# A score tile of key block 3 that spans both query halves, with new order tables

## The chip, the cores and the metric

One NeuronCore of one Trainium2 chip. The metric is device time in microseconds (us) of one execution. The program is straight-line: five engines (TensorE = PE, VectorE = DVE, ScalarE = ACT, GpSimd = POOL, and SyncE = SP, which issues all transfers) each run their own list of instructions in order, and semaphores join them.

## The reference

A block of a transformer on x of 8 x 1024 x 256, all in float32: half a feed-forward part, attention, the same half feed-forward again.

```python
x = x + 0.5 * ffn(layernorm(x))
x = x + attn(layernorm(x))
x = x + 0.5 * ffn(layernorm(x))
```

The feed-forward part is `x @ W.T + b` plus a low-rank part of 8 experts of rank 16, of which a softmax gate keeps the best two. The attention has 16 heads; queries and keys have 16 content dimensions and 32 rotary ones, values have 16. Keys and values come from a latent of 64 that is normalised by its root mean square; scores are scaled by 1/sqrt(48), masked causally and put through a softmax; the output is multiplied by W_o.

## The kernel before, in words

**Tiles.** Tokens are handled in 16 halves of 512 (two per batch). Work before attention (feed-forward, latents, queries and keys) and after it (output projection, feed-forward) is cut into 32 jobs. 30 of them run in lane 0; the second and the last run in lane 1, whose buffers are carved out of `probs` and whose PSUM banks are `o_b` and one bank of `st_b`. Attention is cut into 32 groups (`quads`), each four heads of one batch.

**One group.** `mx` (L807) computes scores with queries on the partitions; DVE takes their row maxima (L998 for tiles on the diagonal, with a mask added, and L1001). When a half's 16 rows of maxima are folded, `mx_turn` transposes them on PE (L813), DVE negates them (L1016), and SP copies them to DRAM (L651) and back (L655) as one extra row of the query operand, the row of shifts. `score` (L775, L777) then computes the transposed scores, keys on the partitions, in two matmuls per head and tile: the second adds the low-order parts of the keys. The row of shifts subtracts each query's maximum. ACT takes the exponential out of `st_b` into the ring `probs` (L884), POOL zeroes the 128 x 128 corner of each tile on the diagonal (L1199), and `pv` (L795) multiplies by the values into `o_b`, four heads side by side. DVE transposes and divides (L1023 to L1036), and SP stores the result (L667).

**The list of score tiles.** `ATT` has for each query half h2 and key block j a tile of the queries from q0 on, n columns: half 0 has n = 512, 384, 256, 128 for j = 0 to 3; half 1 has 512 for j = 0 to 4, then 384, 256, 128. A score matmul is never narrower than 256 columns (`WIDE`): a tile of 128 is computed 256 wide and only its last 128 columns are used. `PV` joins the tiles in pairs, 6 value products a group. `PLACE` gives each tile its place in the ring of 2304 columns, and `BEFORE` the older tile whose value product must be done before it is overwritten.

**What sets the order.** `ORDER` holds a string per engine; each letter takes the next step of one stream (`STREAMS`): on PE S score, X mx, V pv, F mx_turn, P a piece of queries or keys, J and j a job's matmuls, D and d a fill matmul on the identity (L862). The maxima of group g+1 are computed while the scores of group g run. Each engine waits at the head of its own list, so what stands behind a waiting instruction waits too. With two banks, a score waits for the exponential of the score before last (L771), and a maximum matmul for DVE's maximum before last (L806).

**The end.** After the last score of group 31 PE has the y matmuls of the last lane 0 job (L732, L734), the last value product, fill, and then the last job, in lane 1: its output projection is in two parts, the first (L693) on the 128 rows of attention output that the early load (L593) brings, the second (L701) on the rest.

Of the kernel before, what the change touches and what calls it, by code (L numbers as in the profile page):

```python
# [130 lines left out]
def uses(*steps):  # L131

    out = []
    for n, (m, pair, side) in enumerate(UNIT):
# [1139 lines left out]
```

## Time and profile before

| what | value |
|---|---|
| median of 3 runs | 1963.67 us (1953.01 to 1965.78) |
| the profiled execution | 1961.27 us, span 1959.6 us |
| mean granted clock of PE | 0.984 of 2.4 GHz |
| instructions | 32772 |
| busy: DVE, ACT, POOL | 1434.8, 1013.1, 858.1 us |
| moved by DMA | 307.50 MB, mean 157 GB/s |

The span runs from the first to the last instruction of the profiled execution; its time contains 1.7 us around it. Busy times are of that one execution. A PE row's duration runs from its start to the end of its pipeline, so the durations of neighbours overlap, and the starts tell the pace. Idle time of an engine that nobody waits for costs nothing.

### The profile page before, as it was taken

What the parts mean: (1) busy time and instruction counts of PE and PEld (TensorE: products, weight loads), DVE (VectorE), ACT (ScalarE), POOL (GpSimd) and SP (SyncE); (2) the same over time, 40 slices, a digit from 0 to 9 for tenths busy, and PEclk for the clock granted to TensorE, in tenths of its full rate; (3) what the DMA queues carried; (4) which work ended last, traced back from release to release, by engine and by line L of the source; (5) the groups of instructions that cost most, each with busy time, mean ns of one, the idle gap of its engine ahead of it and who ended that gap; (6) DMA issues with size and microseconds to landing.
All of it is one profiled execution on the core that took longest, in us unless ns stands there. A gap on an engine that the chain in (4) does not pass through costs nothing.

```text
span 1959.6 us, 32772 instructions
## 1 busy us (share of the span) xinstructions
PE 1901.9 (97%) x11102; PEld 1337.0 (68%) x11102; DVE 1434.8 (73%) x4570; ACT 1013.1 (52%) x2125; POOL 858.1 (44%) x912
## 2 busy tenths in 40 slices
PE   8789999999999999999999999999999999999997
PEld 7546666767767676776767677677766777677556
DVE  5667777777777777877877777777778778677632
ACT  3435565555555555555555555545555555554551
POOL 3456454543445435355452545535444543432121
PEclk9879999999999999999999999999999999999999
DMA  3775675676775656766666676755677566665611
GB/s 104 199 191 155 166 188 151 151 187 167 176 177 129 178 149 159 200 157 153 162 164 152 179 189 156 179 149 153 153 189 178 143 158 174 167 147 129 133 41 44
DMA packets 169767, 307.50 MB, mean 157 GB/s; under 512 B 15104, under 2 KB 33792, under 8 KB 169600
## 3 DMA queue, kind: packets, MB, share of 16 engines
q1 hardware_dynamic: 169600, 305.40, 62.3%
q8 instruction: 89, 1.46, 0.3%
q14 instruction: 78, 0.64, 0.1%
HBM read 178.99 MB, written 126.22 MB: 156 GB/s over the span
## 4 chain that ended last, share of the span: by engine, by line
PE 86%; DVE 8%; ACT 3%; issue 2%; DMA 1%; POOL 1%; SPq 0%; POOLq 0%; DVEq 0%
PE st_b L775 15%; PE mx_b L807 15%; PE st_b L777 13%; PE o_b L795 13%; PE tp_b L843 5%; PE wj_b L732 5%; PE tp_b L840 4%; PE wj_b L719 3%; PE wj_b L701 3%; PE wj_b L734 2%; PE wj_b L712 2%; PE wj_b L741 1%; PE wj_b L747 1%; DVE mx_b L998 1%; ACT probs L884 1%
## 5 line engine op out<-in xcount | busy, mean ns | idle before, releaser
L884 ACT ACTIVATE probs<-st_b 128x512 f32<-128x512 f32 (+3 forms) x1536 | 699.6, 490 | 582.2 <-PE st_b L777 535.8
L998 DVE CUSTOM_DVE_ANT_0 mx_b<-mx_b,tri 128x256 f32<-128x256 f32 (+3 forms) x1024 | 510.6, 516 | 123.8 <-PE mx_b L807 120.5
L775 PE MATMUL st_b<-st 97*128 97x512 f32 (+2 forms) x1536 | 587.7, 388 | 8.5 <-ACT probs L884 5.0
L807 PE MATMUL mx_b<-st 96*128 96x256 f32 (+2 forms) x1536 | 543.2, 400 | 23.8 <-DVE mx_s L998 14.3
L777 PE MATMUL st_b<-st,k_st 96*128 96x512 f32 (+2 forms) x1536 | 531.2, 350 | 0.0
L1001 DVE TENSOR_REDUCE mx_s<-mx_b 128x1 f32<-128x512 f32 (+1 forms) x512 | 334.3, 653 | 131.8 <-PE mx_b L807 126.5
L1199 POOL TENSOR_SCALAR_AFFINE_SELECT probs<-probs 128x512 f32<-128x512 f32 x256 | 172.2, 677 | 538.1 <-ACT probs L884 538.0
L807 PEld LDWEIGHTS mx_b<-st 96*128 96x128 f32 x1536 | 280.9, 192 | 181.1 <-issue 73.4
L775 PEld LDWEIGHTS st_b<-st 97*128 97x128 f32 x1536 | 291.4, 190 | 123.8 <-issue 54.7
L777 PEld LDWEIGHTS st_b<-st,k_st 96*128 96x128 f32 x1536 | 294.2, 192 | 37.1 <-issue 13.9
L795 PE MATMUL o_b<-probs,v_s 128*17 128x512 f32 (+3 forms) x3072 | 290.3, 496 | 0.0
L795 PEld LDWEIGHTS o_b<-probs,v_s 128*17 128x17 f32 x3072 | 71.1, 97 | 144.8 <-issue 116.1
L998 DVE DVE_READ_ACCUMULATOR2_ANT mx_s<- 128x1 f32 x1024 | 143.6, 140 | 0.0
L527 POOL TENSOR_TENSOR rot<-rot,cos_t 128x512 f32<-128x512 f32 x62 | 80.4, 1297 | 124.4 <-ACT rot L897 124.3
L897 ACT ACTIVATE rot<-tp_b 128x512 f32<-128x512 f32 x124 | 74.1, 598 | 106.8 <-PE tp_b L843 60.6
L732 PE MATMUL wj_b<-w_s,xt 128*128 128x256 f32 x480 | 124.2, 381 | 1.1 <-ACT xn L976 1.1
L1222 POOL TENSOR_TENSOR xa<-xa,hb_s 128x256 f32<-128x256 f32 x120 | 92.7, 799 | 57.7 <-DVE xn L1107 57.7
L843 PE MATMUL tp_b<-stg,wkr_s 128*128 128x512 f32 x240 | 114.3, 598 | 0.8 <-ACT v_s L897 0.6
L1162 DVE SCALAR_TENSOR_TENSOR xa<-wj_b,xa 128x512 f32<-128x512 f32 x60 | 41.5, 692 | 95.0 <-PE wj_b L734 94.9
L732 PEld LDWEIGHTS wj_b<-w_s,xt 128*128 128x128 f32 x480 | 88.5, 190 | 14.4 <-ACT xn L976 3.2
L840 PE MATMUL tp_b<-stg,wq_s 128*128 128x512 f32 x180 | 92.3, 593 | 0.0
L1051 DVE TENSOR_TENSOR lo_t<-rot,hi_t 128x1024 fp32r<-128x1024 f32 x62 | 81.7, 1318 | 9.4 <-ACT hi_t L932 9.2
(198 smaller groups left out, 2332.7 us busy)
## 6 DMA issues: line engine op xcount, KB each, us to landing
st<-q_scratch SPq DMA_DIRECT2D x128, 384.0 KB, 6.0
st<-k_scratch SPq DMA_DIRECT2D x128, 384.0 KB, 8.7
k_st<-k_scratch SPq DMA_DIRECT2D x128, 384.0 KB, 9.2
q_scratch<-hi_t SPq DMA_DIRECT2D x32, 768.0 KB, 3.8
q_scratch<-lo_t SPq DMA_DIRECT2D x32, 768.0 KB, 5.3
k_scratch<-hi_t SPq DMA_DIRECT2D x30, 768.0 KB, 6.1
k_scratch<-lo_t SPq DMA_DIRECT2D x30, 768.0 KB, 4.9
ao_scratch<-o_f SPq DMA_DIRECT2D x252, 32.0 KB, 1.8
```

The costliest lines, as they stand in the source:

```text
L732: nc.tensor.matmul(dst, xt[:, tk, P * kk:P * kk + P], w1_s[:, kk, 0:D], start=(kk == 0), stop=False)
L775: nc.tensor.matmul(dst, k1_st[u][0:SHIFT + 1, a, P * j:P * j + P], q_st[u][0:SHIFT + 1, a, q0:q0 + w], start=True, stop=False)
L777: nc.tensor.matmul(dst, k2_st[0:SHIFT, a, P * j:P * j + P], q_st[u][0:SHIFT, a, q0:q0 + w], start=False, stop=True).then_inc(st_full, 1)
L795: last = nc.tensor.matmul(o_b[32 * a:32 * a + DV + 1, 0, q0 - HALF * h2:q0 - HALF * h2 + n], v_s[g // NQ % 2][:, j, HQ * q + a, :], probs[ ...
L807: nc.tensor.matmul(mx_b[:, m % 2, 0:w], q_st[u][0:SHIFT, a, P * i:P * i + P], k1_st[u][0:SHIFT, a, k0:k0 + w], start=True, stop=True).then ...
L840: last = nc.tensor.matmul(dst, wq_s[:, k, eight], own.stg[:, :, 2 * P:3 * P], start=True, stop=True)
L843: last = nc.tensor.matmul(dst, wkr_s[:, kk, k, eight], own.stg[:, :, P * kk:P * kk + P], start=(kk == 0), stop=(kk == KD - 1))
L884: nc.scalar.activation(probs[:, a, PLACE[s]:PLACE[s] + n], st_b[:, a % 2, HALF - n:HALF], ACT.Exp, scale=SCALE).then_inc(exp_done, 1)
L998: nc.vector.tensor_tensor_reduce(src, src, tri[:, HALF - n:HALF], 1.0, NEG, ALU.add, ALU.max, dst).then_inc(mx_done, 1)
L1001: nc.vector.tensor_reduce(dst, src, AX_X, ALU.max).then_inc(mx_done, 1)
L1199: nc.gpsimd.affine_select(out=d, in_=d, compare_op=ALU.is_ge, fill=0.0, base=0, pattern=[[0, HQ], [1, P]], channel_multiplier=-1).then_inc ...
L1222: last = nc.gpsimd.tensor_tensor(own.xa[:, k, :], own.xa[:, k, :], hb_s[:, :], ALU.add)
```

## The change

The two tiles of key block 3 that stood for half 0 (128 columns, computed 256 wide) and half 1 (512 columns) are cut anew: the first has 256 columns, the last 128 queries of half 0 and the first 128 of half 1, the second the other 384. The second moves up to right behind key block 0's tile of half 1 (`ATT.insert(HT + 1, ...)`). The third value product of a group takes three sets of columns now (`TAKES`): block 0, the second half of the spanning tile, and the 384. The places in the ring follow. The first score of the spanning tile also waits for half 1's row of shifts. The order tables of all five engines are made anew: before, one string for the whole program; now a head, a batch of 4 groups that is repeated 4 times, and a tail. 25 of the 135 fill matmuls are gone, and the last job's projection waits for the reading of `o_b` and the last exponential. Lane 1's carved buffers may reach up to column 1920 of the ring (1792 before).

The diff, with one row of the tables, PE's second, for all:

```diff
--- before.py
+++ after.py
@@ -47,11 +47,18 @@
+BOTH = HT - 1
 ATT = []
 for h2 in range(2):
     for j in range((h2 + 1) * HT):
         q0 = max(P * j, HALF * h2)
-        ATT.append((h2, j, q0, HALF * (h2 + 1) - q0, q0 == P * j))
+        if j == BOTH:
+            q0 += P * h2
+        ATT.append((h2, j, q0, HALF * (h2 + 1) - q0 + (P if j == BOTH and not h2 else 0), q0 == P * j))
+at = [s for s in range(len(ATT)) if ATT[s][0] and ATT[s][1] == BOTH][0]
+ATT.insert(HT + 1, ATT.pop(at))
 NS = len(ATT)
 UNITS = NS * HQ
 DIAG = [s for s in range(NS) if ATT[s][4]]
@@ -66,9 +73,16 @@
     BEFORE.append(max(over))
 PV = [(s, s + 1) for s in range(0, NS, 2)]
 NV = len(PV)
-PV_OF = [p for p in range(NV) for _ in PV[p]]
+TAKES = []
+for p in range(NV):
+    takes = [(s, ATT[s][0], ATT[s][2], min(ATT[s][3], HALF * (ATT[s][0] + 1) - ATT[s][2])) for s in PV[p]]
+    if p == HT // 2:
+        takes.insert(1, (BOTH, 1, HALF, P))
+    TAKES.append(takes)
+PV_OF = [max(p for p in range(NV) if s in [take[0] for take in TAKES[p]]) for s in range(NS)]
 PV_END = [max(p for p in range(NV) if ATT[PV[p][1]][0] == h2) for h2 in range(2)]
@@ -143,122 +157,80 @@
 ORDER = {
     "PE": (
...
-        "JjPJPDPXXPXPXXXPXXJXPXJXXPJXXPXXPFPXXXXXXXXXPXXPJXJXXSSXXSSXXSSPXXSSXXSXSXSVXXPXSSXPXSXSSXXXPXXXXXXXVXXF"
...
+        "JjPJPDPXXPXPXXXPXXJXPXJXXPJXXPXXPFPXXXXXXXXXPXXPJXJXXSSXXSSXXSSPXXSSXXSXSXSVXXPXSXPXXXXXPXXXXXXXXXFXXPXX"
...
 }
@@ -688,6 +660,8 @@
                     late = n == NJ - 1
                     if late and k == 0:
                         pe.wait_ge(ao_early, 16)
+                        pe.wait_ge(o_read, 2 * QUADS)
+                        pe.wait_ge(exp_done, UNITS * QUADS)
                         for tk in range(GT):
                             c = D * (tk % 2)
                             nc.tensor.matmul(wj_of(n, f"wo{tk // 2}")[:, c:c + D], aoc[:, 0, P * tk:P * tk + P],
@@ -762,6 +736,8 @@
                     i = UNITS * g + HQ * s + a
                     if j == 0 and a == 0:
                         pe.wait_ge(shift_in[u][h2], 16 * (g // 2 + 1))
+                    if s == BOTH and a == 0:
+                        pe.wait_ge(shift_in[u][1], 16 * (g // 2 + 1))
                     if j == HT * h2 and a == 0:
                         pe.wait_ge(k2_in[h2], 32 * (g + 1))
                     if g < 2 and s == 0 and a == 0:
@@ -789,11 +765,11 @@
                         pe.wait_ge(o_read, 2 * g + half)
                     if p == 0 and q == 0:
                         pe.wait_ge(tp_free, tp_use("v", 2 * (g // NQ) + 1, 1) + 1)
-                    for s in PV[p]:
-                        h2, j, q0, n, _ = ATT[s]
+                    for s, h2, q0, n in TAKES[p]:
+                        j, place = ATT[s][1], PLACE[s] + q0 - ATT[s][2]
                         for a in range(HQ):
                             last = nc.tensor.matmul(o_b[32 * a:32 * a + DV + 1, 0, q0 - HALF * h2:q0 - HALF * h2 + n],
-                                                    v_s[g // NQ % 2][:, j, HQ * q + a, :], probs[:, a, PLACE[s]:PLACE[s] + n],
+                                                    v_s[g // NQ % 2][:, j, HQ * q + a, :], probs[:, a, place:place + n],
                                                     start=(j == 0), stop=(s == PV[PV_END[h2]][-1]))
                     last.then_inc(pv_done, 1)
                 elif name == "mx":
```

Line numbers of the new kernel are smaller: score is L751 and L753, mx L783, pv L771, mx_turn L789, the fill L838, the projection L667 and L675, y L706 and L708, the v matmuls L832 (L856 before).

**PE, fourth and fifth score tiles of group 16.** 256-column pairs are the tiles of key blocks 2 and 3, 512 those of block 0 for half 1. Before, from the middle of the fourth tile on:

```order
L775 MATMUL st_b<-st 128x256 [waits exp_done]
L777 MATMUL st_b<-st,k_st 128x256
L775 MATMUL st_b<-st 128x256 [waits exp_done]
L777 MATMUL st_b<-st,k_st 128x256
L807 MATMUL mx_b<-st 128x384 [waits mx_done,qk_in11]
L775 MATMUL st_b<-st 128x512 [waits exp_done,shift_in01]
L777 MATMUL st_b<-st,k_st 128x512
L775 MATMUL st_b<-st 128x512 [waits exp_done]
L777 MATMUL st_b<-st,k_st 128x512
L807 MATMUL mx_b<-st 128x256 [waits mx_done]
L807 MATMUL mx_b<-st 128x384 [waits mx_done]
L813 MATMUL tp_b<-ident,mxf 72x128 [waits tp_free,mx_folded]
```

Now, from the first score of the spanning tile on:

```order
L751 MATMUL st_b<-st 128x256 [waits exp_done,shift_in01]
L753 MATMUL st_b<-st,k_st 128x256
L783 MATMUL mx_b<-st 128x512 [waits mx_done]
L751 MATMUL st_b<-st 128x256 [waits exp_done]
L753 MATMUL st_b<-st,k_st 128x256
L783 MATMUL mx_b<-st 128x384 [waits mx_done,qk_in11]
L751 MATMUL st_b<-st 128x256 [waits exp_done]
L753 MATMUL st_b<-st,k_st 128x256
L751 MATMUL st_b<-st 128x256 [waits exp_done]
L753 MATMUL st_b<-st,k_st 128x256
L783 MATMUL mx_b<-st 128x256 [waits mx_done]
L751 MATMUL st_b<-st 128x512 [waits exp_done,shift_in01]
```

The wait for half 1's row (`shift_in01`) stands at the spanning tile's first score now, four heads earlier than before; the tile keeps its 256 columns. Behind these rows the tile of block 3 for half 1, formerly four pairs of 512 three tiles further on, follows with four pairs of 384.

**PE, last scores of group 14 and first of group 15.** `kv_hl`, `kv_lh` are the weights of the v matmuls. Before:

```order
L777 MATMUL st_b<-st,k_st 128x256
L807 MATMUL mx_b<-st 128x256 [waits mx_done] x2
L856 MATMUL tp_b<-kv_hl,kvs 128x256 [waits tp_free]
L856 MATMUL tp_b<-kv_lh,kvs 128x256
L856 MATMUL tp_b<-kv_hl,kvs 128x256
L856 MATMUL tp_b<-kv_lh,kvs 128x256
L775 MATMUL st_b<-st 128x512 [waits exp_done,k2_in0,shift_in10]
L777 MATMUL st_b<-st,k_st 128x512
L775 MATMUL st_b<-st 128x512 [waits exp_done]
L777 MATMUL st_b<-st,k_st 128x512
L807 MATMUL mx_b<-st 128x256 [waits mx_done]
```

Now:

```order
L753 MATMUL st_b<-st,k_st 128x256
L783 MATMUL mx_b<-st 128x256 [waits mx_done] x2
L771 MATMUL o_b<-probs,v_s 17x512 [waits masked]
L771 MATMUL o_b<-probs,v_s 17x512 x3
L771 MATMUL o_b<-probs,v_s 17x384 x4
L751 MATMUL st_b<-st 128x512 [waits exp_done,k2_in0,shift_in10]
L753 MATMUL st_b<-st,k_st 128x512
L751 MATMUL st_b<-st 128x512 [waits exp_done]
L753 MATMUL st_b<-st,k_st 128x512
L783 MATMUL mx_b<-st 128x256 [waits mx_done] x2
```

Behind the two maxima matmuls of 256 columns stood the v matmuls; now a value product of 512 and 384 columns stands there, and the v matmuls come after the next two maxima matmuls.

**PE, the end: last value product and what follows it.** `o_b<-probs,v_s` is the value product, `wj_b` the y matmuls, `wo_s` the projection. Before:

```order
L732 MATMUL wj_b<-w_s,xt 128x256 [waits wj_free]
L732 MATMUL wj_b<-w_s,xt 128x256
L734 MATMUL wj_b<-bt_s,xn 128x256
L732 MATMUL wj_b<-w_s,xt 128x256 x2
L734 MATMUL wj_b<-bt_s,xn 128x256
L795 MATMUL o_b<-probs,v_s 17x256 [waits masked]
L795 MATMUL o_b<-probs,v_s 17x256 x3
L795 MATMUL o_b<-probs,v_s 17x128 x4
L862 MATMUL mx_b<-ident 128x128 [waits mx_done] x26
L693 MATMUL o_b<-wo_s,probs 128x256 [waits ao_early,wj_free_2]
L693 MATMUL o_b<-wo_s,probs 128x256
L693 MATMUL st_b<-wo_s,probs 128x256 x2
```

Now, from the last row of the value product on:

```order
L771 MATMUL o_b<-probs,v_s 17x128 x4
L706 MATMUL wj_b<-w_s,xt 128x256 [waits wj_free]
L706 MATMUL wj_b<-w_s,xt 128x256
L708 MATMUL wj_b<-bt_s,xn 128x256
L706 MATMUL wj_b<-w_s,xt 128x256 x2
L708 MATMUL wj_b<-bt_s,xn 128x256
L706 MATMUL wj_b<-w_s,xt 128x256 [waits wj_free]
L706 MATMUL wj_b<-w_s,xt 128x256
L708 MATMUL wj_b<-bt_s,xn 128x256
L706 MATMUL wj_b<-w_s,xt 128x256 x2
L708 MATMUL wj_b<-bt_s,xn 128x256
L667 MATMUL o_b<-wo_s,probs 128x256 [waits o_read,exp_done,ao_early,wj_free_2]
```

The value product stood behind the y matmuls, followed by 26 fill matmuls; now it stands ahead of them, one fill matmul stands a few rows earlier, and the projection (`o_b<-wo_s,probs`, L667) follows the y matmuls at once.

**SP, the end.** The transfers of the last job. Before:

```order
L600 DMA aoc<-ao_scratch 128x2x512 [waits wj_full,ao_out]
L606 DMA out_y<-xa 128x4x256 [waits wj_free]
L580 DMA probs<-x_scratch 128x1024 [waits stored,pv_done,normed_1_2,stored_2]
L664 DMA probs<-o_f 16x512 [waits o_ready]
L664 DMA probs<-o_f 16x512 x3
L593 DMA probs<-ao_scratch 128x512 [waits pv_done,ao_out]
L594 DMA probs<-ao_scratch 64x512
L606 DMA out_y<-probs 128x4x256 [waits wj_free_2]
```

Now:

```order
L572 DMA aoc<-ao_scratch 128x2x512 [waits wj_full,ao_out]
L552 DMA probs<-x_scratch 128x1024 [waits stored,pv_done,normed_1_2,stored_2]
L565 DMA probs<-ao_scratch 128x512 [waits pv_done,ao_out]
L566 DMA probs<-ao_scratch 64x512
L636 DMA probs<-o_f 16x512 [waits o_ready]
L636 DMA probs<-o_f 16x512 x3
L578 DMA out_y<-xa 128x4x256 [waits wj_free]
L578 DMA out_y<-probs 128x4x256 [waits wj_free_2]
```

The load of x for the last job and the two early loads (`probs<-ao_scratch`) have moved ahead of the four small transfers (`probs<-o_f`), and lane 0's last store behind them.

## Rows read from the trace of the kernel before

**Rows 1.** Page, part 1: busy us, share of the span, instructions of each engine.
```profile
PE 1901.9 (97%) x11102; PEld 1337.0 (68%) x11102; DVE 1434.8 (73%) x4570; ACT 1013.1 (52%) x2125; POOL 858.1 (44%) x912
```

**Rows 2.** Page, part 4: chain that ended last, share of the span by engine.
```profile
PE 86%; DVE 8%; ACT 3%; issue 2%; DMA 1%; POOL 1%; SPq 0%; POOLq 0%; DVEq 0%
```

**Rows 3.** Groups by form, PE: shapes, count | busy us, mean ns | idle before.
```profile
L775 PE MATMUL st_b<-st 97*128 97x512 f32 x768 | 327.7, 427 | 4.5 <-ACT probs L884 2.2 <-issue 1.2
L777 PE MATMUL st_b<-st,k_st 96*128 96x512 f32 x768 | 306.2, 399 | 0.0
...
L775 PE MATMUL st_b<-st 97*128 97x384 f32 x256 | 98.6, 385 | 0.3 <-ACT probs L884 0.2
...
L777 PE MATMUL st_b<-st,k_st 96*128 96x384 f32 x256 | 86.8, 339 | 0.0
```

**Rows 4.** Time line, PE, middle: start us, us, engine, line, what, count.
```profile
1002.42 0.40 PE L775 MATMUL st_b<-st 97*128 97x512 f32 x1
...
1003.35 0.34 PE L807 MATMUL mx_b<-st 96*128 96x384 f32 x1
...
1007.91 0.84 PE L795 MATMUL o_b<-probs,v_s 128*17 128x256 f32 x16
...
1013.28 1.91 PE L795 MATMUL o_b<-probs,v_s 128*17 128x512 f32 x16
...
1028.83 0.34 PE L775 MATMUL st_b<-st 97*128 97x384 f32 x1
...
1029.53 0.40 PE L847 MATMUL tp_b<-kvs,kv_hl 128*128 128x512 f32 x1
...
1049.53 1.70 PE L795 MATMUL o_b<-probs,v_s 128*17 128x512 f32 x16
```

**Rows 5.** Time lines; last row a stretch: us, busy of five engines, PEclk, DMA.
```profile
750.89 0.39 PE L807 MATMUL mx_b<-st 96*128 96x256 f32 x1 [1.80 <-DVE mx_s L998]
...
1213.43 0.39 PE L807 MATMUL mx_b<-st 96*128 96x256 f32 x1 [0.57 <-DVE mx_s L998]
...
1675.83 0.38 PE L807 MATMUL mx_b<-st 96*128 96x256 f32 x1 [1.77 <-DVE mx_s L998]
...
747.34 0.69 DVE L1132 TENSOR_TENSOR k1m<-iota,ixf 128x32 f32<-128x32 f32 x1
...
1944.65 0.19 DVE L1132 TENSOR_TENSOR probs<-iota,probs 128x32 f32<-128x32 f32 x1
...
747.25 2.10 POOL L1222 TENSOR_TENSOR xa<-xa,hb_s 128x256 f32<-128x256 f32 x3
...
751.80:755.20 3.40, 3.40 (x14) 1.66 (x16) 2.15 (x11) 1.79 (x3) 1.64 (x2) 0.50 1.00 297
```

**Rows 6.** Time line, PE, first group of heads.
```profile
151.02 0.49 PE L807 MATMUL mx_b<-st 96*128 96x512 f32 x1 [0.46 <-DVE mx_s L998]
```

**Rows 7.** Time lines of the end: POOL, PE, and the DMA queue's issues.
```profile
1915.91 0.63 POOL L1199 TENSOR_SCALAR_AFFINE_SELECT probs<-probs 128x512 f32<-128x512 f32 x1 [1.40 <-ACT probs L884]
...
1915.83 1.10 PE L732 MATMUL wj_b<-w_s,xt 128*128 128x256 f32 x4 [0.54 <-ACT xn L976]
...
1921.17 0.84 PE L795 MATMUL o_b<-probs,v_s 128*17 128x256 f32 x16
...
1930.17 1.10 PE L693 MATMUL o_b<-wo_s,probs 128*128 128x256 f32 x4 [2.15 <-DMA probs<-ao_scratch]
...
1924.39 2.51 SPq L664 DMA_DIRECT2D probs<-o_f  x4
```

**Rows 8.** Last group: transposed maxima, copy of the row, first score; landings of L651.
```profile
1871.29 0.30 PE L813 MATMUL tp_b<-ident,mxf 128*72 128x128 f32 x1
...
1873.44 0.56 SPq L655 DMA_DIRECT2D st<-shift_scratch  x1
...
1882.41 0.28 PE L775 MATMUL st_b<-st 97*128 97x256 f32 x1
...
DMA to landing us min/median/max: 1.3/2.7/7.5
```

More of the change, by code:

```diff
@@ new lines @@
+        "EEEEEJEEEEEEEEEEEEEEEEEJEEJEEJEEJEECEECEJCHEEEECEECEEJJEEJEEJEECEEJEEHEECEEJEECEEEEEEEECEECEECEEEEEHEEEE"
+        "EJEEJEECJEEJEEJEECEEEEJEECEEEEHEEEEEEEEEEEEJEEJEEJEEJEECEECEEJEECEEHEEEECEECEECJEEJEEJEEJEEHJEEEECEECEEJ"
+        "EEEEEEEECEEEECEECEEEEEEHEEECEECEEJEEJEEJEEJEECEEHJEEEE",
+        "EEEEEJEEEEEEEEEEEEEEEEEJEEJEEJEEJEECEECEJCHEEEECEECEEJJEEJEEJEECEEJEEHEECEEJEECEEEEEEEECEECEECEEEEEHEEEE"
+        "EJEEJEECJEEJEEJEECEEEEJEECEEEEHEEEEEEEEEEEEJEEJEEJEEJEECEECEEJEECEEHEEEECEECEECJEEJEEJEEJEEHJEEEECEECEEJ"
@@ L211 @@
+        "EEEEEEEECEEEECEECEEEEEEHCEECEECEEEEEEHEEEEEEEEEEEEEEEEJEEJEEJEEJEEJEEEEEEEEEEEEJEEEEEEEEEEEEEEEEEEEEEEEE"
+        "EEEEJEEJEEJEEJEEJEEEEEEEEEEEEJEEEEEEEEEEEEEEEEEEEEEEEEEEEEEEEEEEEEEEEEEEEEEEEEEEEEEEEEEEEEEEEEEEEEEEEEEE"
+        "EEEEEEEEEEEEEEEEEEEEEEEEEEEEEEEEEEEEJJEEJJEEJEEEEEEJjjjjjj",
     ),
@@ L238 @@
[L238 to L241 removed]
+        "MMMMLMMJMJMMMMMMMLMMMMMMLMMMMMMMMMLMMfMMMMMMLMMMnMMMMMLMMfnMMMMJLMMJMMoMMooMMoMLMMMMMMJMMJLMMJMMJMMJMJMM"
+        "LMfnJMMJMMJJMMLJJJMMJoJoJMMoMMoMJMMMMfMMJnMMJMJMMLMMJLMMJMMoJoMMooMMMMMMMMMMMMMMLLMMfnJMMJMMMMJMJJMMoJMM"
+        "ooMMoMMLMLfJMMJnMMMMMoMMooMMoMMLMMMLMMMMMMMMMMMMMMMMLfJnMMJJJJJJJMMJJMMLMMoMMoMMooMMMMfMJMMLLMnMoMMoJMMM"
@@ new lines @@
+        "oMMoJJMMJMMMJMMJMMMMMMMMMMMJMMJfMMnJMMoMMoooJMMJMMJMMJJMMMMLMMfMLMMJnMMJoMMoMoMMoMMMMMMJMJJJJMMJMMJLMJLJ"
+        "MMJMMMMMMfJnMMJMMMMMMoMMooMMoMMLMMfMMMJMMJMJLMMJnMMJoMMoMMooMMMMMMMJMJJJJMMJJJJJMMMMLMMLJMMfJnMMJJJMMMMJ"
+        "MMJMMoMMooMoMMMMfJMMJnMMMJMMMMMMLJMMoMMoooLMMJJMMJJMMJMJMMMMLMMMMMMfJLJnJMMJJJJJJJMMMMMMMMJMMJMMoMofoMMo"
+        "nMMMJMMJMJMMLoMMoooMMJMMLMMJMMMMMMMMMMMMJMJMJfJLJMMJLnJJM",
+        "MJJMMooMoMoMJMMJMMJJMMJMMfMJMMnJMMoMMooMMoMMMMJMMJMMMMJMMLJMMJMMJJMMJLMMJJMMfnMMJMMJMMJJLJJJMMJJJMMLMMoM"
@@ new lines @@
+        "MoooJMMfJMMnMMMMMMMMLMMJMMJoJMMooJMMJMMoMMLMMMMMMJJJJJMMJJJJJMMfnMMMMMMLJMMLJJMMJoMMJMMoJJMMoMMfoMnMMMMM"
+        "JMMJMMMMJMMLJMMoooLMMoJMMJJJMMJJMMLMMMMMMMfJJJJLnMMJJJJJJMMMMMMMMJMMJMMoMofoMMonMMMMMJMJMMLJMMoooMMoJMML"
+        "MMJMMMMMMMMMMMMJMJMJfJLJMMJLnJJM",
+        "MJJMMooMoMoMJMMJMMJJMMJMMfMJMMnJMMoMMooMMoMMMMJMMJMMMMJMMLJMMJMMJJMMJLMMJJMMfnMMJMMJMMJJLJJJMMJJJMMLMMoM"
+        "MoooJMMfJMMnMMMMMMMMLMMJMMJoJMMooJMMJMMoMMLMMMMMMJJJJJMMJJJJJMMfnMMMMMMLJMMLJJMMJoMMJMMoJJMMoMMfoMnMMMMM"
@@ L262 @@
+        "sJqaJkuussaqkuusJsqkaJJssuauqkuusksqJJassauuqkusu",
+        "sqakJsJsJaqkuussquuaksJsJuaquksqsJuukasJsJuuaqkuusksqJJassauuqkusu",
+        "sqakJsJsJaqkuussquuaksJsJuaquksqsJuukasJsJuuaqkuusksqJJassauuJqkususqakssaJJJqkssqakssaJJqksqsakssaksksa"
+        "aJjjaJj",
     ),
```

145 lines of the change are left out of this document (39 added, 106 removed).

## Prediction

> **What bounds the kernel now.** I read the engine shares first: TensorE (PE) is busy 97% of the span [rows 1]. The chain that ended last says the same: 86% of it is PE work, 8% VectorE (DVE), 3% ScalarE (ACT) [rows 2]. So a column removed on PE is worth its own time wherever PE isn't waiting in that stretch. Where PE does wait I looked at its time line: a recurring spot in the middle [rows 5], the first group of heads [rows 6], and the last 45 us, one long chain [rows 7].
>
> **Score columns.** Key block 3 had two score tiles: 128 useful columns for query half 0, computed 256 wide, and 512 for half 1. Now they are 256 and 384 wide. The first costs what it did; the second loses 128 columns in 2 matmuls for each of 4 heads and 32 groups: 128 pairs (L775, L777) go from the 512 to the 384 form. By mean durations a pair falls from 427 + 399 to 385 + 339 ns, so 102 ns [rows 3], times 128 = 13.1 us. By starts in the time line, two 512 pairs take 1003.35 - 1002.42 = 0.93 us, two 384 pairs 1029.53 - 1028.83 = 0.70 us [rows 4]: 0.115 us a pair, times 128 = 14.7 us. I take 14.0: durations overlap between matmuls and starts don't, but not every pair stands back to back. The lower end is 0, if PE then waits for exponentials or maxima instead.
>
> **Exp, mask, value product.** The exponentials keep their total of columns (128 + 512 becomes 256 + 384) and their count, and hide behind PE, which is at 97%: nothing; without that cover it would still be nothing. The mask still works on 128 columns of each diagonal tile. The value product of key block 3 for half 1 is now two sets, 128 columns out of the first tile and 384 out of the second: 128 more matmuls in the program, the same columns. Does a split cost? 512 + 512 columns take 1.91 us, 512 + 384 take 1.70, 256 + 128 take 0.84 [rows 4]. So 128 columns are worth 0.21 us, and 1.70 - 4 x 0.21 = 0.86 us agrees with the 0.84 us of the group that has a 128-column set in it: a short set costs its columns alone, 0. The upper end charges each of the 32 groups one step of 0.21 us more, +6.7 us.
>
> **The new wait.** Key block 3's first tile now waits for half 1's row of shifts, one tile earlier than it was needed, with all of PE behind it. In the last group, where the way is shortest, the maxima are transposed at 1871.29, the row's copy is issued at 1873.44 (0.56 us), and that tile starts at 1882.41 [rows 8]. A write of these maxima lands after 2.7 us in the median; if the row takes as long it is there at 1876.7, 5.7 us early. Cost 0; the upper end is rival C.
>
> **First group of heads.** There the tile can't stand before the shift any more. The order puts its four score pairs and one value product behind the transposition. They lay in a stretch in which PE waited for DVE's maxima (0.46 us at 151.02, [rows 6]); now they stand where PE is full: 4 pairs of 256 columns (a 512 pair of 0.465 us less 2 x 0.115 = 0.235 us) plus 0.84 us = +1.8 us. Ends 0 and +5: PE may also be granted the low clock there, as after the waits of rows 5.
>
> **The end.** The y matmuls of the last lane 0 job (from 1915.83) stand ahead of the last value product, though its operand was masked by 1915.91 + 0.63 = 1916.54; it runs at 1921.17 [rows 7]. Behind it come DVE's division, four small issues from 1924.39 (2.51 us), the early load issued behind them, and at 1930.17 the output projection, which waited 2.15 us for that load. The new order has the value product first, the y matmuls in place of 26 fill matmuls, and the early load ahead of the four. Step by step: value product 1916.6 to 1917.4; the four issues 2.4 us later, as now (1921.17 + 0.84 to 1924.39), so 1919.8 to 1922.3, and the last one lands some 2 us after its issue, near 1923.8; the early load is issued near 1918.5 and took 1930.17 - 1926.90 = 3.3 us, so it is there by 1921.8. PE: y matmuls 1917.4 to 1922.7 (they took 1921.17 - 1915.83 = 5.3 us), then at once the projection, against 1930.17: -7.5 us, of which I count 7.4. All behind it is the same. Ends -4 (the four transfers land 3 us later) and -8.
>
> **The recurring spot.** At 750.89 PE has waited 1.80 us for DVE [rows 5], which is late because small routing operations take long (L1132 0.69 us at 747.34, 0.19 us at 1944.65) while GpSimd adds biases (2.10 us from 747.25). Right after it PE is granted 0.50, which is 1.2 GHz, for 3.4 us: 1.7 us lost. Such a wait is there five times, every 232 us, from 750.89 to 1675.83; the least, 0.57 us at 1213.43, had no low clock behind it. At four times 1.80 + 1.7 and once 0.57 it costs some 14 us.
> The page SBUF — State Buffer of the Trainium skill, section Who interferes with whom, says that a DVE instruction with two SBUF inputs contends with a GpSimd instruction that reads SBUF, and that the later one is blocked. The trace agrees: both sides have two SBUF inputs here.
> In the new order DVE has a similar run, but behind the two maxima matmuls PE has a value product of 1.70 us, where four v matmuls of 256 columns (0.12 us each, half a 256 pair) stood. That covers 1.2 of the 1.8 us and leaves a wait like that at 1213.43. If nothing like it arises elsewhere the gain is some 12 us; a new table can make such spots anew, which its order alone doesn't tell. I take half, -6; ends -14 and +8 (two or three new ones a batch).
>
> **Sum.** -14.0 - 7.4 + 1.8 - 6 = -25.6 against the profiled execution's 1961.3: 1935.7. That execution lies 2.4 us under the median of 1963.67, so I say 1938; its own range is 1930 to 1946.
>
> **Rivals.**
> A: nothing is won at the recurring spots: -19.6, so 1944; with new ones 1952. For it: the same runs of routing operations are still there. Against: more cover at the known spot.
> B: the scores' gain turns into waits for maxima and exponentials: the sum without the 14.0, 1952. For it: [rows 5] and [rows 6] show PE paced by DVE. Against: those are single places; PE is 97% busy.
> C, the other side: the shift row is late, at the first score of key block 3 in each group. The longest landing seen is 7.5 us [rows 8]; a copy out and a copy back of that length make at most 17.7 us from transposition to tile (2.15 + 7.5 + 0.56 + 7.5), 6.6 more than the 11.1 us of the last group. At 1.5 us in each of 32 groups it is +48: 1986. It decides from 25.6 / 32 = 0.8 us a group. Against: the median landing leaves 5.7 us.
> D: PE falls to the low clock at the end, now that 26 fill matmuls are gone. The y matmuls of the last job (5.3 us) and some 3 us of transpositions and products on that chain would double: +8, 1946. Against: y matmuls fill the place, and the wait of 2.15 us goes.
> The page TensorE: Matmul & The Clock Gate of the Trainium skill, section HAM oscillation, says that a kernel whose PE idles between bursts drops to half rate and pays for it each time; by that rule taking fill away is a risk, and the time would be D's. The trace agrees at the recurring spots.
>
> **Chances.** Forecast 0.54, A 0.24, B 0.10, D 0.07, C 0.05. A measurement of this kernel can tell about 1% from no change, so faster means under 1944.0. That takes 0.52 of the forecast's 0.54, 0.12 of A, 0.02 of B and 0.03 of D, rounded to 0.70; same is 0.25, slower 0.05 (C). The range is 1926 (the spots all gone) to 1954 (A with new ones, and B).
>
> **What would show it.** The 384-column form of both score matmuls counts 384 instead of 256, the 512 form 640, with means as they are. The projection starts right behind the y matmuls, some 29 us before the end, with no wait for the early load. No wait of 1.8 us every 232 us and no clock of 0.50 in the middle. No wait ahead of key block 3's first tile. I am wrong if PE's waits and low clocks in the middle grow, or if that tile waits for a transfer.

## The result and the profile after

The changed kernel takes 1933.22 us (median of 6 runs, 1930.2 to 1939.6) against 1963.82 for the kernel before beside it (6 runs): ratio 0.9859, 95% interval 0.9836 to 0.9882. Forecast were 1938 and 1926 to 1954. Its profiled execution took 1934.2 us, span 1932.5. Two later groups of runs gave 0.987 (0.9839 to 0.9901) and 0.9861 (0.9837 to 0.9884). Three single executions of later runs (3659.8 us in e0, 3040.9 in e2, 2111.6 in e6) were slow ones and are left out of ratios and medians.

I cut both spans at the same marks, the starts of the last score matmul of groups 0, 7, 27 and 31. Two views of the stretches, first the kernel before, then the changed one (us, length, then busy time and count of PE, PEld, DVE, ACT, POOL, then PE's granted clock, DMA share, GB/s):

```profile
0.00:190.80 190.80, 164.70 (x787) 115.36 (x788) 126.39 (x397) 83.07 (x144) 93.51 (x100) 0.91 0.58 161
190.80:573.50 382.70, 379.79 (x2242) 262.56 (x2240) 295.53 (x931) 212.66 (x449) 180.99 (x188) 0.99 0.67 169
573.50:1731.40 1157.90, 1143.92 (x6754) 809.29 (x6752) 886.57 (x2816) 618.23 (x1315) 543.15 (x566) 0.99 0.67 166
1731.40:1914.80 183.40, 178.49 (x1080) 118.62 (x1080) 114.22 (x387) 95.57 (x210) 34.71 (x51) 0.99 0.45 98
1914.80:1959.60 44.80, 34.98 (x249) 31.22 (x247) 12.14 (x45) 3.59 (x9) 5.73 (x8) 0.97 0.15 48
```

```profile
0.00:192.20 192.20, 165.27 (x794) 114.57 (x795) 126.51 (x397) 82.44 (x143) 93.14 (x97) 0.91 0.59 159
192.20:574.80 382.60, 376.79 (x2299) 262.40 (x2297) 296.18 (x928) 214.52 (x451) 183.91 (x191) 1.00 0.68 169
574.80:1712.80 1138.00, 1129.16 (x6913) 810.01 (x6913) 888.89 (x2821) 622.89 (x1315) 536.92 (x566) 1.00 0.66 168
1712.80:1896.60 183.80, 178.70 (x1109) 120.38 (x1107) 113.93 (x384) 95.96 (x209) 33.62 (x51) 0.98 0.46 102
1896.60:1932.50 35.90, 29.55 (x202) 26.01 (x200) 12.14 (x45) 3.86 (x9) 6.45 (x9) 0.99 0.18 59
```

The gain is in two places: the middle, groups 8 to 27, 1157.9 to 1138.0 us (PE busy 14.8 us less, idle 5.1 less), and the end, 44.8 to 35.9. Groups 1 to 7 and 28 to 31 gain nothing, although scores got narrower there too. The forms of the scores, which answer to [rows 3] (count | busy us, mean ns | idle before):

```profile
L753 PE MATMUL st_b<-st,k_st 96*128 96x512 f32 x640 | 254.6, 398 | 0.0
...
L751 PE MATMUL st_b<-st 97*128 97x384 f32 x384 | 144.4, 376 | 1.1 <-ACT probs L860 1.0
...
L753 PE MATMUL st_b<-st,k_st 96*128 96x384 f32 x384 | 130.1, 339 | 0.0
```

128 of each moved from 512 to 384 columns, at the means of before (the first score matmul has 376 ns for 385). The recurring spot, which answers to [rows 5]: PE's time line and the same stretch of clock.

```profile
751.76 0.76 PE L783 MATMUL mx_b<-st 96*128 96x256 f32 x2 [0.38 <-DVE mx_s L974]
```

```profile
751.80:755.20 3.40, 3.40 (x22) 3.16 (x23) 2.81 (x12) 2.34 (x6) 1.37 (x2) 1.00 1.01 230
```

The wait is 0.37 or 0.38 us at all five spots, where it was 1.80, 1.77, 0.57, 1.52 and 1.77, and the clock stays 1.00. The end, which answers to [rows 7] (PE, then SyncE's issues):

```profile
1904.15 1.03 PE L667 MATMUL o_b<-wo_s,probs 128*128 128x256 f32 x4
...
1905.88 1.03 PE L675 MATMUL o_b<-wo_s,probs 128*128 128x256 f32 x4
```

```profile
1899.50 0.39 SPq L565 DMA_DIRECT2D probs<-ao_scratch  x1
...
1901.32 2.50 SPq L636 DMA_DIRECT2D probs<-o_f  x4
1905.07 0.40 SPq L578 DMA_DIRECT2D out_y<-xa  x1
```

The projection (L667) starts right behind the y matmuls, 7.6 us behind the last score instead of 15.4, and 28.4 us before the end.

### The profile page after: what moved, and what is told of

Read it like the earlier page. It is cut to its first block, busy times and chain, and to the rows that moved or that the text cites. A ratio compares the mean times of both kernels' runs of the same rounds, so it can differ in the third digit from the quotient of the medians.

```text
span 1932.5 us, 33217 instructions
## 1 busy us (share of the span) xinstructions
PE 1879.5 (97%) x11308; PEld 1333.4 (69%) x11308; DVE 1437.6 (74%) x4570; ACT 1019.7 (53%) x2125; POOL 854.0 (44%) x912
## 4 chain that ended last, share of the span: by engine, by line
PE 84%; DVE 7%; DMA 4%; ACT 2%; issue 2%; POOL 1%; SPq 1%; POOLq 0%; DVEq 0%
PE st_b L751 14%; PE mx_b L783 14%; PE st_b L753 12%; PE o_b L771 12%; PE tp_b L819 6%; PE wj_b L706 5%; PE tp_b L816 4%; PE wj_b L693 3%; PE wj_b L675 3%; PE wj_b L708 2%; PE wj_b L686 2%; DMA st<-k_scratch 2%; PE wj_b L715 1%; PE wj_b L721 1%; DVE mx_b L974 1%
## 5 line engine op out<-in xcount | busy, mean ns | idle before, releaser
L751 PE MATMUL st_b<-st 97*128 97x512 f32 (+2 forms) x1536 | 577.3, 381 | 7.3 <-ACT probs L860 5.7
L783 PE MATMUL mx_b<-st 96*128 96x256 f32 (+2 forms) x1536 | 550.6, 402 | 22.0 <-DVE mx_s L974 12.4
L753 PE MATMUL st_b<-st,k_st 96*128 96x512 f32 (+2 forms) x1536 | 523.0, 345 | 0.0
L783 PEld LDWEIGHTS mx_b<-st 96*128 96x128 f32 x1536 | 282.2, 192 | 167.3 <-issue 68.7
L751 PEld LDWEIGHTS st_b<-st 97*128 97x128 f32 x1536 | 291.1, 190 | 121.4 <-issue 52.9
L753 PEld LDWEIGHTS st_b<-st,k_st 96*128 96x128 f32 x1536 | 293.3, 191 | 28.8 <-issue 9.1
L771 PE MATMUL o_b<-probs,v_s 128*17 128x512 f32 (+3 forms) x3328 | 286.7, 466 | 0.7 <-POOL probs L1175 0.7
L771 PEld LDWEIGHTS o_b<-probs,v_s 128*17 128x17 f32 x3328 | 77.7, 97 | 139.6 <-issue 107.4
L706 PE MATMUL wj_b<-w_s,xt 128*128 128x256 f32 x480 | 123.9, 380 | 0.6 <-ACT xn L952 0.6
L706 PEld LDWEIGHTS wj_b<-w_s,xt 128*128 128x128 f32 x480 | 88.2, 190 | 12.8 <-ACT xn L952 2.0
```

The source lines that it names most:

```text
L706: nc.tensor.matmul(dst, xt[:, tk, P * kk:P * kk + P], w1_s[:, kk, 0:D], start=(kk == 0), stop=False)
L751: nc.tensor.matmul(dst, k1_st[u][0:SHIFT + 1, a, P * j:P * j + P], q_st[u][0:SHIFT + 1, a, q0:q0 + w], start=True, stop=False)
L753: nc.tensor.matmul(dst, k2_st[0:SHIFT, a, P * j:P * j + P], q_st[u][0:SHIFT, a, q0:q0 + w], start=False, stop=True).then_inc(st_full, 1)
L771: last = nc.tensor.matmul(o_b[32 * a:32 * a + DV + 1, 0, q0 - HALF * h2:q0 - HALF * h2 + n], v_s[g // NQ % 2][:, j, HQ * q + a, :], probs[ ...
L783: nc.tensor.matmul(mx_b[:, m % 2, 0:w], q_st[u][0:SHIFT, a, P * i:P * i + P], k1_st[u][0:SHIFT, a, k0:k0 + w], start=True, stop=True).then ...
```

## The experiments

Twelve kernels, each timed beside the kernel before. By stage of the one profiled execution of each (us; marks as above, worked out from the starts of the last score matmul):

| kernel | to group 0 | 1 to 7 | 8 to 27 | 28 to 31 | last score to end | ratio to before (95%) |
|---|---|---|---|---|---|---|
| before | 190.8 | 382.7 | 1157.9 | 183.4 | 44.8 | 1 |
| changed | 192.2 | 382.6 | 1138.0 | 183.8 | 35.9 | 0.9859 |
| changed again (e0) | 193.5 | 383.7 | 1139.2 | 184.1 | 35.9 | 0.987 (0.9839 to 0.9901) |
| changed again (e11) | 193.1 | 382.1 | 1139.0 | 181.6 | 35.9 | 0.9861 (0.9837 to 0.9884) |
| e1 wide tile | 193.1 | 383.0 | 1148.3 | 184.4 | 36.1 | 0.9935 (0.9912 to 0.9958) |
| e3 new tables, old tiles | 195.7 | 384.9 | 1147.7 | 182.6 | 35.9 | 0.9935 (0.9916 to 0.9954) |
| e9 old tables, new tiles | 192.9 | 383.1 | 1143.6 | 183.8 | 46.3 | 0.9953 (0.9935 to 0.997) |
| e2 before, new end | 191.8 | 379.5 | 1156.3 | 180.5 | 36.2 | 0.9951 (0.9932 to 0.997) |
| e8 changed, old SyncE end | 192.6 | 379.2 | 1140.6 | 184.0 | 47.2 | 0.9903 (0.9883 to 0.9923) |
| e7 changed, no fill | 194.5 | 381.0 | 1139.8 | 184.6 | 40.9 | 0.9905 (0.9879 to 0.9932) |
| e4 before, spot reordered | 191.1 | 379.5 | 1156.4 | 182.3 | 45.7 | 0.9984 (0.9966 to 1.0001) |
| e5 before, few bias adds | 192.4 | 381.1 | 1147.2 | 185.8 | 45.8 | 0.995 (0.9934 to 0.9967) |
| e6 before, split product | 190.6 | 381.5 | 1157.4 | 185.4 | 43.9 | 0.9957 (0.9939 to 0.9975) |
| e10 hybrid tables | 195.2 | 382.9 | 1140.2 | 183.4 | 35.9 | 0.9864 (0.9839 to 0.9888) |

The repeats show the grain: the three traces of the changed kernel agree within 1.2 us in the middle and 0.1 at the end, but within 1.6 and 2.5 in groups 1 to 7 and 28 to 31. e7 and e8 run the same instructions up to the last 40 us, and with them the spreads are 2.6 in the middle (1138.0 to 1140.6), 4.5 in groups 1 to 7 (379.2 to 383.7) and 3.0 in 28 to 31. The one profiled execution can also lie off its kernel's median: e6's is 9 us above it, e5's 4 above, e2's 4 below.

**The width alone (e1).**

```diff
-                    w = max(n, WIDE)
+                    w = HALF if (h2, j) == (1, BOTH) else max(n, WIDE)
```

> The changed kernel once more, as the measure for the others of its group, on the same chip. Every theory: 1933 us, as measured.

> The changed kernel, in which the second score tile of key block 3 is computed 512 columns wide again, into the same tile of PSUM; exponentials, masks, value products and all tables stay. It gives back only the PE columns that the change removed: 128 pairs of 128 columns. My theory (PE bounds wherever it doesn't wait, 0.115 us a pair by starts, 0.102 by durations): +13 to +15 us over the changed kernel, 1946 to 1948. Rival, the columns were hidden behind waits for maxima and exponentials: under +5 us, at most 1938, and the gain lies in the tables. Rival, columns are dearer than their own time because of the clock: over +20.

Measured 1946.2 us against 1935.5 in the same group (0.9935 against 0.987 and 0.9861): 11 to 15 us. In the middle it is 1148.3 against 1138.7, the mean of three: 9.6 us for 80 pairs, 0.12 us a pair, what the starts of [rows 4] say. The 48 pairs outside are 5.5 us by that price. Of this some 2 us show: 383.0 against 382.8 in groups 1 to 7 (381.8 with e7 and e8), 184.4 against 183.2 in the last four. But the repeats spread by more than what is sought, and the timed runs have room for the full price, so the traces can't tell what these pairs are worth.

**Tables and tiles apart (e3, e9).** e3 takes the old tile list with the new tables; e9 the new tiles with the old tables from the second group on.

```diff
-ATT.insert(HT + 1, ATT.pop(at))
...
-        takes.insert(1, (BOTH, 1, HALF, P))
...
-                    if s == BOTH and a == 0:
-                        pe.wait_ge(shift_in[u][1], 16 * (g // 2 + 1))
```

> The order tables of the changed kernel with the tiles of the kernel before: key block 3 is 128 columns for query half 0 and 512 for half 1, five steps apart as before, each with its own value product, no wait for half 1's shifts ahead of it. Against the kernel before it is the tables alone, against the changed kernel the tile list alone. My theory: the tables bring the end (-7.8 in the traces) and the recurring spots (-11 in the traces), less some 5 lost in the first eight groups: -14 to -17 against before, 1947 to 1950, and 14 slower than the changed kernel. Rival, the tables only fit the new tile list and gain nothing with the old one: 1960 or more.

> The new tiles and the new wait on the order tables of the kernel before: only the first letters of each table (up to some 145 us, the first group of heads) are the changed kernel's, since there the old order can't stand with the new wait; everything behind is the old order, the old end included. My theory: the scores' gain is the tiles' own and comes in the middle (10 us between the last scores of groups 7 and 27, as the wide tile gave back), the recurring spots and the old end stay: 1946 to 1950, -10 to -14 against before. Rival, the new tiles need the new order (the fourth tile and the product that takes from it collide with the old one): over 1955. Rival C of the prediction, the shift row is late: a wait ahead of the fourth tile, over 1960.

e3 gains 12.7 us by its ratio, a little under the 14 to 17 expected: 8.9 at the end, 10.2 in the middle, less some 8 ahead of it (195.7 for 191.3 and 384.9 for 380.9, means given below). e9 gains 9 us, for 10 to 14 expected: 14.3 in the middle, nothing at the old end. The two middles add up to 24.5, but both edits together give 19.2, so part of both gains is the same one. In e3 the recurring spots are gone (waits of 0.37 us), so the tables alone take them away. In e9 the old table has them in their mild form, four times of five, a form that the kernel before and e2 show too (0.57 us); whether the new tiles bring it about isn't shown:

```profile
751.17 0.38 PE L830 MATMUL mx_b<-st 96*128 96x256 f32 x1 [0.54 <-DVE mx_s L1021]
...
1664.18 0.38 PE L830 MATMUL mx_b<-st 96*128 96x256 f32 x1 [1.76 <-DVE mx_s L1021]
```

e9 also shows rival C in small. Under the old order the fourth tile's first score waits for half 1's row of shifts (`st<-shift_scratch`) in group 3, and by 0.72 us once more in group 30 (at 1829.72):

```profile
323.10 0.40 PE L798 MATMUL st_b<-st 97*128 97x256 f32 x1 [2.17 <-DMA st<-shift_scratch]
```

e10, which has the old order there too, waits 1.98 us at the same place (325.20). So it is the new order that makes the new wait free.

**The spot's mechanism (e5, e4).** In e5 GpSimd adds the bias to one column in the five jobs whose adds run at the spots; in e4 DVE's 1024-column operation on the low parts of queries and keys (`L`, which the expectation calls a routing operation) stands behind two maxima instead of ahead of them.

```diff
-                    last = nc.gpsimd.tensor_tensor(own.xa[:, k, :], own.xa[:, k, :], hb_s[:, :], ALU.add)
+                    c = slice(0, 1 if g in (11, 15, 19, 23, 27) else D)
+                    last = nc.gpsimd.tensor_tensor(own.xa[:, k, c], own.xa[:, k, c], hb_s[:, c], ALU.add)
```

```diff
+for g in range(12, QUADS - 3, 4):
+    at = steps.index(("mx", g, 5))
+    text[at - 1:at + 2] = "MML"
```

> The kernel before, in which GpSimd adds the bias to one column of 256 instead of all in the jobs whose adds run at the recurring spots (11, 15, 19, 23, 27), so part of the computation is left out. DVE's order and PE's are as before. Theory, DVE is late at the spots because its routing operations are slowed from 0.19 to 0.69 us while GpSimd adds: with the adds gone the operations are 0.19 us, no wait at the spots and no low clock, -9 to -14 us. Rival, the routing operations are late by their place in DVE's order, or by the order of the chain behind them: they stay as long as they are or the wait stays within 0.3 us, within 2 us of before.

> The kernel before with one edit of DVE's order at each of the five recurring spots (groups 12, 16, 20, 24 and 28): the routing operation of the low-rank part that stood ahead of two maxima now stands behind them. My theory, the spot costs its wait and the low clock behind it: the waits of 1.5 to 1.8 us and four stretches at clock 0.50 go, -9 to -14 us against before, 1950 to 1955. Rival, the wait only moves to the next pair of maxima: all of it still there, -3 to +2 us. Rival, the wait goes but PE pays for the same work later, with no low clock: -7 (four times 1.7).

DVE at the spot, before and then in e5, whose order is the same:

```profile
747.34 0.69 DVE L1132 TENSOR_TENSOR k1m<-iota,ixf 128x32 f32<-128x32 f32 x1
747.95 0.77 DVE L1133 TENSOR_TENSOR k2m<-iota,ixf 128x32 f32<-128x32 f32 x1
748.64 1.80 DVE L1051 TENSOR_TENSOR lo_t<-rot,hi_t 128x1024 fp32r<-128x1024 f32 x1
750.36 0.42 DVE L998 CUSTOM_DVE_ANT_0 mx_b<-mx_b,tri 128x256 f32<-128x256 f32 x1
```

```profile
746.71 0.19 DVE L1132 TENSOR_TENSOR k1m<-iota,ixf 128x32 f32<-128x32 f32 x1
746.82 0.18 DVE L1133 TENSOR_TENSOR k2m<-iota,ixf 128x32 f32<-128x32 f32 x1
747.03 1.22 DVE L1051 TENSOR_TENSOR lo_t<-rot,hi_t 128x1024 fp32r<-128x1024 f32 x1
748.17 0.42 DVE L998 CUSTOM_DVE_ANT_0 mx_b<-mx_b,tri 128x256 f32<-128x256 f32 x1
```

From L1132 to the maximum behind L1051 it is 3.02 us before (747.34 to 750.36) and 1.46 in e5 (746.71 to 748.17). No wait of 0.45 us or more is left at the spot, PE has full clock all through the middle, and it is 10.7 us shorter; 9.8 by the ratio. So contention with GpSimd's adds makes the spot. The page SBUF — State Buffer of the Trainium skill, section Who interferes with whom, says that a DVE instruction with two SBUF inputs contends with a GpSimd instruction that reads SBUF; the trace agrees, with 0.69 and 0.77 us beside the adds and 0.19 and 0.18 without them. e4 missed: the operation takes 1.65 us in its new place as well, and PE waits for the maxima behind it instead (first row; the second is a further wait that the kernel before doesn't have):

```profile
749.24 0.45 PE L814 MATMUL mx_b<-st 96*128 96x384 f32 x1 [0.97 <-DVE mx_s L1005]
...
997.21 0.56 PE L814 MATMUL mx_b<-st 96*128 96x384 f32 x2 [0.89 <-DMA st<-k_scratch]
```

The wait is 0.96 or 0.97 us at all five spots, and no low clock follows in the middle (busy 1140.7 against 1143.9). But idle time grows from 14.0 to 15.7, so 1.5 us are won (3.1 by the ratio, whose interval reaches to none). That is nearest to its first rival, the wait moves, though it moves in a smaller form; the new waits farther behind (0.89 us at 997.21, 0.80 at 1228.42, 1.23 at 1467.10) are not traced to the edit.

**The end (e2, e8, e7).** e2 puts the new end on the kernel before (the letters, and the two new waits ahead of the projection):

```diff
-PE "JJV" + 26 "d" + "jj"    DVE "JJoooo"    SP "aaJJjajj"
+PE "VJJjj"                  DVE "ooooJJ"    SP "aaJjjaJj"
```

> The kernel before with the end of the changed kernel alone: on PE the last value product ahead of the y matmuls of the last lane 0 job, and that job's matmuls in place of 26 fill matmuls; on DVE the division of the last output ahead of that job's two steps; on SP the early load ahead of two of the four small transfers. My theory: the projection starts right behind the y matmuls, -7.5 to -9 us against before, about 1955. Rival, the low clock comes at the end once the fill matmuls are gone (rival D of the prediction): 0 to -1. Rival, the gain needs the other tables too (ACT and GpSimd at the end): under -4.

Ratio 0.9951, so -9.6 us; from the last score to the end 36.2 for 44.8 us. The end's gain is these few letters. They also take away a low clock that the old end has in some executions: in e4, e5 and e9 it follows the wait of 2.4 to 3.0 us for the early load, and from the projection's start to the last matmul's it is 25.6 us, for 23.9 in the kernel before and e6 and 23.8 in e2 and the changed kernel. In e4:

```profile
1924.89 1.10 PE L700 MATMUL o_b<-wo_s,probs 128*128 128x256 f32 x4 [2.40 <-DMA probs<-ao_scratch]
...
1927.40 1.91 PE L708 MATMUL o_b<-wo_s,probs 128*128 128x256 f32 x4
```

e8 gives SyncE its old letters back in the changed kernel ("aaJjjaJj" to "aaJJjajj"), e7 leaves out the 43 steps of fill behind the scores (the expectation counts 44).

> The changed kernel with the old order of SyncE at the very end: the four small transfers of the last output ahead of the early load, which PE's projection waits for. By the prediction's steps the early load then issues 2.5 us later, near 2.5 us behind the start it has now, and takes 3.3 us: PE waits for it 1.5 to 3 us, but the projection's later half waits for the four transfers in any case, so that of this 0 to 3 us reach the end: +1.5 expected. Rival, the whole gain at the end (8.8 us from the last score in the traces) hangs on this order: +5 or more. Rival, none of it: under +0.5.

```profile
1904.88 0.40 SPq L582 DMA_DIRECT2D out_y<-xa  x1
...
1905.87 2.86 SPq L640 DMA_DIRECT2D probs<-o_f  x4
1908.83 0.53 SPq L569 DMA_DIRECT2D probs<-ao_scratch  x1
```

```profile
1912.21 2.05 PE L671 MATMUL o_b<-wo_s,probs 128*128 128x256 f32 x4 [8.08 <-issue]
```

My number was wrong: 47.2 us from the last score to the end, 11.3 more than the changed kernel, and 8 us by the ratios; the rival "the whole gain hangs on this order" holds. I had counted the four small issues (2.5 us) and overlooked the store of the last lane 0 job, the first J, which stands ahead of them. It waits until DVE has read that job's y matmuls, which the change has moved behind the value product, so SyncE stands until 1904.88 with the early load behind it. That lands 3.4 us after 1908.83; PE waited 8.08 us (the view names "issue") and starts at half clock, 2.05 us for four matmuls against 1.03. Without the move on SyncE the moves on PE and DVE lose at the end: 47.2 us against 44.8 before, or 43.9 to 46.3 in the five traces with the old end.

> The changed kernel without its 44 fill matmuls at the end. My theory from the stretches at clock 0.50 in both traces: PE falls to the low clock in the projection's wait for the last transfers, and what follows runs at half speed: +3 to +8 us over the changed kernel. Rival, the last 20 us wait for transfers and chains of small operations on other engines, and the clock of PE matters little there: within 1 us.

1939.6 us, 0.9905 against 0.9861 and 0.987: 7 to 9 us by the ratios, 5.0 in the trace (40.9 against 35.9). One of the 11 timed executions took 1962.65 us at clock 0.935 and raises the ratio. What fill is worth is seen in the first matmuls behind an idle stretch of e7 (the same four take 0.63 us in the changed kernel, at 1913.36), and in views of stretches of e7, then of the changed kernel:

```profile
1916.66 1.08 PE L686 MATMUL o_b<-ident,probs 128*128 128x128 f32 x4 [5.59 <-DVE probs L1083]
```

```profile
1926.00:1934.00 8.00, 6.91 (x18) 5.40 (x19) 0.25 (x1) 0.60 (x1) 0.17 (x1) 0.50 0.00 0
```

```profile
1914.00:1922.00 8.00, 7.25 (x63) 6.85 (x62) 2.72 (x23) 2.11 (x5) 3.12 (x5) 1.00 0.00 0
1922.00:1932.00 10.00, 5.80 (x28) 4.67 (x26) 1.38 (x2) 0.60 (x1) 0.00 (x0) 1.00 0.15 52
```

After idle stretches of 5.6 and 4.7 us PE runs at 0.50; with fill in them it doesn't, and the clock stays 1.00. The trace so agrees with what the page TensorE: Matmul & The Clock Gate of the Trainium skill, section HAM oscillation, says of idling between bursts.

**Splitting a value product (e6).**

```diff
-                        for a in range(HQ):
+                        for lo, n in ((0, P), (P, n - P)) if (h2, j) == (1, 1) else ((0, n),):
...
+                            for a in range(HQ):
```

> The kernel before, in which one value product set of 512 columns of every group (key block 1, query half 1) is done as two sets, 128 and 384 columns, as the changed kernel does for key block 3: 128 more matmuls, the same columns. My theory, a short set costs its columns alone: 0, within 2 us of before. Rival, each split costs one step of 0.21 us in 32 groups: +6.7.

The trace says 0: 1157.4 against 1157.9 us in the middle. The timed runs say -8 us, which neither theory has. The profiled execution, 1960.5 us, is the slowest of e6's nine; the others took 1947.7 to 1956.5. The loss of 6.7 is out by both; why the timed runs are faster stays open. The spots are a candidate only: in the profiled execution all five have the long wait (1.79 or 1.80 us), at a mean clock of 0.986, and the eight others have 0.988 to 0.991. No trace shows what their spots were.

**Groups 1 to 7 (e10).** The changed kernel's tables up to some 145 us and from some 600 us on, the old ones between; no diff, since only letters move.

> The changed kernel once more, as the measure for the others of its group. Every theory: 1933 to 1937 us, 25 us under before.

> The changed kernel with the old order tables in groups 1 to 8 alone (from some 145 us on; the first letters and all behind some 600 us are the changed kernel's). The last score of group 7 came at 575 to 577 us in traces of the changed kernel and at 581 with its tables and the old tiles, but at 571 to 573 in those of before and its variants. My theory, the new tables lose this in groups 1 to 7 by their order: the last score of group 7 at 569 to 572 and 4 to 6 us under the changed kernel, 1929 to 1931. Rival, the new tiles lose it there (fewer columns, so PE waits for maxima and exponentials): within 1.5 us of the changed kernel.

Missed: 0.9864, the changed kernel's time, and its last score of group 7 came at 578.1 us. Groups 4 to 7 alone took 215.1 us in both e9 and e10, against 216.3 to 218.3 in the traces of the changed kernel, e7 and e8, so the old order looks better there; groups 1 to 3 took 168 against 163.0 to 165.9 and gave that back. In e10 1.98 us of this is the wait for the row of shifts at 325.20, with a clock of 0.57 in the 3.4 us behind it. A join behind group 3 wasn't tried.

## Why the prediction was right, step by step

- **Scores, -14.** The price a pair is right (0.12 us by e1, 0.115 forecast). In the middle 80 pairs gave 9.6 us. For the 48 others the traces show some 2 of 5.5 us, less than they can tell, and the timed runs put the whole at 11 to 15. So the term is 9.6 in the middle and between that and the full 14 as a whole. That PE waits instead in the other stages, rival B in small, would fit but isn't shown. I hadn't priced by stage.
- **Exp, mask, split product, 0.** Right: the value product has 3328 rows in the profile for 3072, and 286.7 us busy for 290.3, and e6 has no loss in its trace.
- **The new wait, 0.** Right. In the last group, the tightest, the transposition is at 1854.63 and the fourth tile's first score close behind 1864, with no idle time ahead of it. In the three traces of the changed kernel the row is late once, by 0.23 us (375.39 in e0); waits of 0.33 us ahead of the tile in five groups are for ACT's exponential. Rival C did show where the old order meets the new wait (2.17 us in e9, 1.98 in e10), in one or two groups and not in 32.

```profile
1854.63 0.27 PE L789 MATMUL tp_b<-ident,mxf 128*72 128x128 f32 x1
...
1864.12 0.39 PE L751 MATMUL st_b<-st 97*128 97x256 f32 x1
```

- **First group, +1.8.** +1.6: 192.9 (mean of three) against 191.3 (mean of before, e2, e4, e5 and e6).
- **The recurring spot, -6.** Right in direction, short in size. The middle lost 19.2 us, 9.6 of it by the width, so 9.6 are the spots; e5 takes 10.7 by removing their cause alone. I had halved my 12 for new spots, and the middle has none. In groups 1 to 7, where I hadn't looked, the wait at 303.91 was 1.39 us before (at 301.51). The one at 430.71 is not the order's alone: it is 0.69 and 0.72 us in the two repeats and under 0.45 in e7 and e8. PE's time line, then the clock behind the first:

```profile
303.91 0.83 PE L783 MATMUL mx_b<-st 96*128 96x256 f32 x2 [1.93 <-DVE mx_s L974]
430.71 0.38 PE L783 MATMUL mx_b<-st 96*128 96x256 f32 x1 [1.50 <-DVE mx_s L974]
```

```profile
303.80:307.20 3.40, 3.29 (x12) 1.29 (x16) 2.91 (x11) 0.92 (x2) 1.06 (x1) 0.50 1.03 244
```

  The contention itself has not gone. In every trace with the new tables DVE's 1024-column operation takes 1.82 to 1.84 us at all five spots. But the new order puts two maxima ahead of the two small operations, and a value product behind PE's two maxima matmuls (first spot of the changed kernel, DVE, then PE):

```profile
746.40 1.83 DVE L1027 TENSOR_TENSOR lo_t<-rot,hi_t 128x1024 fp32r<-128x1024 f32 x1
...
748.82 0.63 DVE L1108 TENSOR_TENSOR k1m<-iota,ixf 128x32 f32<-128x32 f32 x1
749.38 0.66 DVE L1109 TENSOR_TENSOR k2m<-iota,ixf 128x32 f32<-128x32 f32 x1
```

```profile
746.90 1.70 PE L771 MATMUL o_b<-probs,v_s 128*17 128x512 f32 x16
```

  So the slowed run is cut in two and covered, not shortened. The cover that I gave as the reason is there, but how much is its and how much DVE's order's no run tells apart.
- **Groups 1 to 7.** Missing in the sum: 382.8 us against 380.9 before (means of the traces named; 381.8 with e7 and e8), where 28 pairs should have taken 3.2 off. Some 4 or 5 us are lost, in traces of one order that differ by 3 to 4.5. The new order may have 2 of them (groups 4 to 7 in e10); the rest isn't settled.
- **The end, -7.4.** -8.9: the projection starts 7.8 us earlier, as worked out (7.5). Most of the other 1.1 is no part of the change: from DVE's last operation to the end it is 4.37 us in the trace of the kernel before and 3.41 to 3.43 in all the others, with the old end or the new. Rival D fell, because the fill that stayed is enough; e7 shows that it would have come without.
- **The sum.** By stages 1.6 + 1.9 - 19.2 - 0.2 - 8.9 = -24.8 in the traces, -25.6 forecast; by the ratios it is -28, and -25.5 and -27 in the two repeats. It fits partly by luck: the spots' 3.6 us too little and the end's 1.5 stood against the scores' 4.4 too much (9.6 for 14) and the 1.9 of groups 1 to 7.

## What to carry to other kernels

Price a narrower operation by stage: here its columns paid in full where the engine had no other wait behind it, and in the stages with more waits the traces couldn't show that they did. When work is moved on one engine, walk the issue queue in the same place: one store that waits for the moved work holds every load behind it. Before reordering around a late engine, look at what slows its operation; moving one slowed operation (e4) moved the wait, taking the contention away (e5) removed it, and splitting the slowed run and covering it (the change) hid it. A new wait that is free in one order need not be in another.
